# Unpacking of 4-bit weight codes: four operations in one step, or one behind each of four steps

## The reference, cut to what is computed

```python
xn = layernorm(x)
Wg, Wu, Wd = dequant(gate), dequant(up), dequant(down)   # 4-bit codes, two to an int32 word,
                                                         # scale per block of 32
gate, up = xn @ Wg.T, xn @ Wu.T                          # 2048 x 2048 each
g = tanh(0.79788 * (gate + 0.044715 * gate**3)) * gate * 0.5 + gate * 0.5
ffn = (g * up) @ Wd.T
attn = causal_attention(xn; 16 heads of 128)             # with its q, k, v, o projections
out = x + attn + ffn
```

## Time and profile before

| | us |
|---|---|
| median of 3 runs | 1382.64 |
| lowest, highest | 1381.21, 1383.4 |
| span of the traced execution | 1378.4 |
| feed-forward loop in it, with its start | about 42 to 345 |
| PE busy in it | 1301.3 |
| DVE, ACT, POOL busy in it | 960.6, 802.6, 792.9 |

### The profile page before, as it was taken

How to read it: one execution, slowest core, us unless ns; L and a number is a source line. 1 busy time by engine, 2 the same in 40 slices (tenths; PEclk the granted TensorE clock), 3 DMA queues, 4 the chain that set the end, 5 groups by cost and what they waited for, 6 DMA issues and landing times.

```text
span 1378.4 us, 25462 instructions
## 1 busy us (share of the span) xinstructions
PE 1301.3 (94%) x7628; PEld 1091.0 (79%) x7628; DVE 960.6 (70%) x1489; ACT 802.6 (58%) x1720; POOL 792.9 (58%) x799
## 2 busy tenths in 40 slices
PE   3899999998989999999999999999999999999996
PEld 2677777776668888878888887788888868888885
DVE  7777778887756666677665767766666686676665
ACT  3556555555366666645666665466666636666663
POOL 5566666666065576543656675266655715566563
PEclk9899999999999999999999999999999999999999
DMA  4000000000200000011000001100000020000003
GB/s 94 14 7 12 13 11 11 11 26 0 81 15 19 18 11 12 11 54 31 12 11 23 11 11 30 53 11 11 11 19 15 11 61 12 22 11 11 11 23 122
DMA packets 68144, 33.07 MB, mean 24 GB/s; under 512 B 17552, under 2 KB 68112, under 8 KB 68112
## 3 DMA queue, kind: packets, MB, share of 16 engines
q10 hardware_dynamic: 42544, 23.01, 5.8%
q1 hardware_dynamic: 25568, 9.66, 2.7%
HBM read 30.57 MB, written 2.10 MB: 24 GB/s over the span
## 4 chain that ended last, share of the span: by engine, by line
PE 68%; DVE 2%; issue 2%; ACT 1%; POOL 1%; DMA 1%; ACTq 0%; DVEq 0%; POOLq 0%
PE ps L43 19%; PE ps L45 18%; PE ps L44 18%; PE ps L1106 9%; PE ps L1045 2%; PE ps L1096 1%; DVE q_all L933 1%; DMA q_all<-in_x 1%; DVE neg_max L989 0%; POOL probs L878 0%; DVE v_lo L906 0%; DVE wq_lo L917 0%; POOL inv_sum L874 0%; POOL q_lo L854 0%; ACT pt_hi L781 0%
## 5 line engine op out<-in xcount | busy, mean ns | idle before, releaser
L951 DVE TENSOR_TENSOR pt_lo<-ps,pt_hi 128x512 fp32r<-128x512 f32 (+3 forms) x384 | 204.0, 552 | 275.4 <-ACT pt_hi L781 272.8
L874 POOL TENSOR_TENSOR inv_sum<-row_sum,minus_one 128x1 f32<-128x1 f32 x256 | 141.5, 553 | 379.2 <-ACT probs L795 379.2
L878 POOL TENSOR_TENSOR probs<-probs,inv_sum 128x128 f32<-128x128 f32 (+7 forms) x256 | 294.1, 1149 | 20.0
L795 ACT ACTIVATE probs<-ps,neg_max 128x128 f32<-128x128 f32 (+7 forms) x256 | 190.1, 743 | 115.7 <-DVE neg_max L989 111.6
L989 DVE TENSOR_REDUCE neg_max<-ps 128x1 f32<-128x128 f32 (+7 forms) x256 | 191.8, 749 | 4.6 <-PE ps L1096 2.4
L781 ACT ACTIVATE pt_hi<-ps 128x512 fp32r<-128x512 f32 (+3 forms) x384 | 173.4, 488 | 34.9 <-PE ps L1106 34.8
L44 PE MATMUL ps<-pt_lo,v_hi 128*128 128x256 f32 (+1 forms) x640 | 177.6, 278 | 0.0
L45 PE MATMUL ps<-pt_hi,v_lo 128*128 128x256 f32 (+1 forms) x640 | 177.6, 277 | 0.0
L43 PE MATMUL ps<-pt_hi,v_hi 128*128 128x256 f32 (+1 forms) x640 | 173.8, 272 | 0.7 <-DVE pt_lo L951 0.7
L1106 PE MATMUL ps<-ident,probs 128*128 128x128 f32 x1152 | 171.0, 275 | 1.6 <-POOL probs L878 0.6
L43 PE MATMUL ps<-k_hi,q_hi 128*128 128x512 f32 (+3 forms) x384 | 142.7, 372 | 2.6 <-DVE q_lo L942 2.2
(11 more groups left out here) (106 smaller groups left out, 3140.5 us busy)
## 6 DMA issues: line engine op xcount, KB each, us to landing
wq_in<-in_wq ACTq DMA_DIRECT2D x67, 128.0 KB, 2.2
kv_in<-in_wk ACTq DMA_DIRECT2D x33, 128.0 KB, 2.3
kv_in<-in_wv ACTq DMA_DIRECT2D x33, 128.0 KB, 2.2
wo_in<-in_wo ACTq DMA_DIRECT2D x33, 128.0 KB, 2.0
q_all<-in_x SPq DMA_DIRECT2D x1, 2048.0 KB, 8.8
out<-q_all SPq DMA_DIRECT2D x8, 256.0 KB, 2.3
raw<-in_gate SPq DMA_DIRECT2D x18, 64.0 KB, 1.8
raw<-in_up SPq DMA_DIRECT2D x18, 64.0 KB, 1.9
```

The source lines that it names most:

```text
L795: nc.scalar.activation(probs[:, t % 4, 0:width], flat(S[t % 2])[:, 0:width], ACT.Exp, bias=neg_max[:, t:t + 1], accum_out=row_sum[:, t:t + ...
L874: nc.gpsimd.tensor_tensor(inv_sum[:, t:t + 1], row_sum[:, t:t + 1], minus_one[:], ALU.pow).then_inc(inv_done, 1)
L878: nc.gpsimd.tensor_tensor(row, row, inv_sum[:, t:t + 1].to_broadcast([P, (i + 1) * P]), ALU.mult).then_inc(probs_done, 1)
L951: nc.vector.tensor_tensor(pt_lo[where], T[at % 2][:, 0:blocks * P].rearrange("p (a b) -> p a b", b=P), pt_hi[where].bitcast(F32), ALU.subt ...
```

## The change

`integers` becomes four calls of `integer(j, slot, part)`: parts 0 and 1 make `mag` (low and high code), parts 2 and 3 `sgn`. In the loop the call of `integers` is gone; in place of it each step ends with one part, behind `hid` and ahead of `w_lo`: part (kk + 1) % 4 of chunk it * 4 + 3 + (kk + 1) // 4. So part 0 of a chunk is behind step kk % 4 == 3, parts 1 to 3 behind the three steps after it. Part 0 of chunk 3 stands ahead of the loop; the last step has none, so the last 16 steps become a third copy of `body` on DVE and the loop has two turns. A new semaphore, `mag_done`, is counted up behind part 1, `ints_done` behind part 3. ACT's `over4` (part 0 of `linear`) waits for `mag_done`, its `half_sign` (part 3) for `ints_done`. DVE waits ahead of part 0 for the codes and for ACT's third operation on the last `mag`, and ahead of part 2 for the fourth, on the last `sgn`. No other queue's text changes; what is computed is the same.

```diff
--- before.py
+++ after.py
@@ -140,8 +140,8 @@
         offsets_set, stats_done, mean_done, eps_done, rstd_done, rows_done = (
             sem(s) for s in ("offsets_set", "stats_done", "mean_done", "eps_done", "rstd_done", "rows_done"))
         xt_done, xt_hi_done, xt_lo_done = sem("xt_done"), sem("xt_hi_done"), sem("xt_lo_done")
-        ints_done, linear_done, vals_done, w_rows_done = (
-            sem(s) for s in ("ints_done", "linear_done", "vals_done", "w_rows_done"))
+        mag_done, ints_done, linear_done, vals_done, w_rows_done = (
+            sem(s) for s in ("mag_done", "ints_done", "linear_done", "vals_done", "w_rows_done"))
         wt_done, wt_hi_done, wt_lo_done = sem("wt_done"), sem("wt_hi_done"), sem("wt_lo_done")
         gu_done, sq_done, inner_done, th_done, gated_done, hid_done = (
             sem(s) for s in ("gu_done", "sq_done", "inner_done", "th_done", "gated_done", "hid_done"))
@@ -286,6 +286,8 @@
 
                 for part in parts:
                     if part == 0:
+                        act.wait_ge(mag_done, j + 1)
+                    if part == 3:
                         act.wait_ge(ints_done, j + 1)
                     wait(act, vals_done, j * 3 - (2, 2, 1, 0)[part])
                     if part == 0:
@@ -355,16 +357,28 @@
 
         @block.vector
         def _(dve):
+            def integer(j, slot, part):
+
+                if part == 0:
+                    dve.wait_ge(raw_in[slot], (j >> 1) * 48 + 48)
+                    wait(dve, linear_done, j * 4 - 1)
+                if part == 2:
+                    wait(dve, linear_done, j * 4)
+                dst, mask = ((mag, 7), (sgn, 8))[part // 2]
+                pairs = dst[:].rearrange("p (k two) -> p k two", two=2)
+                if part % 2 == 0:
+                    ins = nc.vector.tensor_scalar(pairs[:, :, 0], raw[:, slot, :], mask, None, ALU.bitwise_and)
+                else:
+                    ins = nc.vector.tensor_scalar(pairs[:, :, 1], raw[:, slot, :], 4, mask,
+                                                  ALU.logical_shift_right, ALU.bitwise_and)
+                if part == 1:
+                    ins.then_inc(mag_done, 1)
+                if part == 3:
+                    ins.then_inc(ints_done, 1)
+
             def integers(j, slot):
-
-                dve.wait_ge(raw_in[slot], (j >> 1) * 48 + 48)
-                wait(dve, linear_done, j * 4)
-                for dst, mask in ((mag, 7), (sgn, 8)):
-                    pairs = dst[:].rearrange("p (k two) -> p k two", two=2)
-                    nc.vector.tensor_scalar(pairs[:, :, 0], raw[:, slot, :], mask, None, ALU.bitwise_and)
-                    last = nc.vector.tensor_scalar(pairs[:, :, 1], raw[:, slot, :], 4, mask,
-                                                   ALU.logical_shift_right, ALU.bitwise_and)
-                last.then_inc(ints_done, 1)
+                for part in range(4):
+                    integer(j, slot, part)
 
             def weights_low(j, slot):
                 dve.wait_ge(wt_hi_done, j + 1)
@@ -431,7 +445,7 @@
                     last = nc.vector.tensor_tensor(acc[:, :, cols], D, acc[:, :, cols], ALU.add)
                 last.then_inc(acc_done, 1)
 
-            def body(it, first):
+            def body(it, first, last=False):
                 for kk in range(BODY):
                     s, k1 = kk % 2, it * BODY + (kk + 1)
                     dve.wait_ge(sq_done, k1)
@@ -440,8 +454,6 @@
                                                    ).then_inc(inner_done, 1)
                     if kk % 2 == 1 and not (first and kk == 1):
                         add_down((kk - 3) // 2 % TC, it * GROUPS + (kk - 1) // 2, first and kk < 2 * TC + 3)
-                    if kk % 4 == 0:
-                        integers(it * 4 + (3 + kk // 4), (3 + kk // 4) % 2)
                     dve.wait_ge(th_done, k1)
                     nc.vector.scalar_tensor_tensor(gated[:, s, :], th[:, s, :], 1.0, G[s], ALU.add, ALU.mult
                                                    ).then_inc(gated_done, 1)
@@ -451,11 +463,16 @@
                                                    ALU.mult).then_inc(hid_done, 1)
                     if first and kk == 0:
                         xn_low(3)
+                    if not (last and kk == BODY - 1):
+                        m = (kk + 1) // 4
+                        integer(it * 4 + (3 + m), (3 + m) % 2, (kk + 1) % 4)
                     if kk % 4 == 3:
                         weights_low(it * 4 + (2 + kk // 4), (2 + kk // 4) % 4)
+            integer(3, 1, 0)
             body(0, True)
-            with dve.Fori(1, NJ // 4) as it:
+            with dve.Fori(1, NJ // 4 - 1) as it:
                 body(it, False)
+            body(NJ // 4 - 1, False, True)
             add_down(TC - 1, NJ // 4 * GROUPS, False)
 
         @block.tensor

```

## The result

The changed kernel takes 1361.56 us (median of 4 runs, 1361.07 to 1362.04) where the kernel before takes 1382.9 beside it: ratio 0.9849, 95% interval 0.9837 to 0.9861. The traced execution has a span of 1359.7 us where that of before has 1378.4: 18.7 us less. The forecast was 1362.5 us, from 20.1 us less.

The account below looks back on a forecast made before the run. PE was taken as the bound, so a pass gains only what PE waits. 15 passes x 1.25 = 18.8 us, plus 1.3 at the start, gives 20.1: 1382.64 - 20.1 = 1362.5 us, range 1359.5 to 1371.

Parts of the forecast that it names:

- a distance of 4.2 us: Median of the runs, 1382.64, above the traced span, 1378.4, before the change; the forecast left it unchanged.
- PE waits for `hid` once a pass: Feed-forward loop, step 2: PE's wait costs 1.25 us of an 18.66 us pass; without it 17.41.
- Why the unpackings are long: DVE ahead of `hid`: two unpackings take 1.47 and 2.00 us against POOL's `hid_lo` and `vals`, 0.35 when free.
- The pass laid out by hand: Times of the new pass on each engine from step 0's start, with PE at 0, 4.19, 8.38, 13.14 and 17.41.
- The step that failed: Part 0 behind step 3: held by `vals` to about 3.34, `w_lo` about 3.27, `inner` 4.24 instead of 3.63.
- the loop's term: Feed-forward loop: the stall goes in every pass, 15 passes x 1.25 = 18.8 us.
- The start: First steps: part 0 of chunk 3 loses to `vals`, yet `hid` comes at 45.65 instead of 46.93; gain 1.3, bounds 0 to 1.7.
- Rival 1's margin: Step 1: later `mag_done` uses up 1.17 us, half the gain returns, 1371.9; together with its worst end 0.15.
- Rival 4: Part 1 blocked through `hid_lo` and `w_rows` to 11.14; 2.05 lost for 1.25 won per pass, 1394.6; chance 0.06.
- The Trainium skill's rule: DVE and POOL's shared ports: speaks against spreading, since each part now meets POOL; dearest pass is four full blocks.

Follow-up runs that it names:

- run 1: The changed kernel with `w_lo` ahead of part 0 behind step 3: 1359.97 us, ratio to the kernel before 0.9844.
- run 4: The kernel before, unpackings in their old place, POOL's third operation on `vals` (the sign) cut to 8 of 768 columns: 1356.77 us, one run.
- run 6: The kernel of run 1 with part 0 of chunk 3 between the first `inner` and `gated` instead of ahead of the loop: 1359.31 us, 0.9837.
- The repeat: The changed kernel, unaltered, measured once more for a comparison on one chip: 1362.48 us, ratio to the kernel before 0.9858.
- with six: The changed kernel with six added statistics operations on DVE ahead of part 1 in every pass but the start: 1374.23 us, one run.
- with nine: The changed kernel with nine added statistics operations on DVE ahead of part 1 in every pass but the start: 1390.29 us, one run.
- run 2: The kernel before with all four unpackings as one block, one count, moved behind `hid` of step 0: 1364.09 us, ratio 0.9866.
- run 3: The block of run 2 with two counts, one behind `mag` and one behind `sgn`: 1363.08 us, ratio to the kernel before 0.9865.

## Why the prediction was right, step by step

The mechanism and the size of the gain were right; that the time came within 0.9 us has luck in it. The trace lost 18.7 us, 1.4 less than the 20.1 forecast. Against that, the forecast kept a distance of 4.2 us from the span to the median, and measured it is 1.9 (1361.56 and 1359.7). Where an execution's own time and span are both known, they lie 1.7 to 1.9 apart, so the traced execution of the kernel before took about 1380.3 us by this estimate and was faster than its median. The two errors take most of each other away.

- *PE waits for `hid` once a pass, worth 1.25 us, and the next latest is PE itself.* Right but for `w_lo` (below): 17.41 us in a pass without a late start, and the floor that runs 1, 4 and 6 share is a loop of 273.7: 292.66 - 273.7 = 18.96 us, 15 times 1.26.
- *Why the unpackings are long: they stand against POOL.* Right; run 4 cuts the POOL operation short and the unpacking is short (0.36 instead of 2.00).
- *The pass laid out by hand.* Measured from 196.98: part 0 at 2.66 (laid out 2.66), `w_lo` 3.27 (3.27), `inner` 4.14 (4.24), `hid` 6.23 (6.33), part 1 6.83 (6.93), `over` 8.21 (8.2), `hid` of step 1 11.23 (11.23), part 3 15.20 (15.2). A pass of a steady loop can be laid out from start-to-start distances.
- *The step that failed:* "`w_lo` starts about 3.27 [...] Cost on DVE 0.61 us", which went on to `inner` and stopped there. `w_lo` has a second reader: PE's gate/up of step 1 waits for it whenever it takes up a new chunk, and that starts at 4.19, when `w_lo` ends at 4.2. The forecast priced who is queued behind the held operation on its engine and not who waits for it. Mis-sized by it is the loop's term: 15 x 1.25 = 18.8, of which 17.6 came; the seven starts behind `w_lo` cost 1.39 us by run 1, and the wait itself was worth 19.0.
- *The start.* Forecast 1.3, measured 1.29 (13.59 to 12.30). `inner` came at 43.41 where 43.56 was laid out, `hid` at 45.51 (45.65). In this trace PE's slow stretch covers the late `mag_done`, as the forecast had it: `hid` is issued at 51.51, and step 3 starts at 52.65, more than 0.74 behind. The repeat has 11.95: its slow stretch lies earlier, and PE waits 0.95 us for `hid` in the first step 3. The exact hit has some luck in it.
- *The third copy of `body` on DVE* cost nothing: PE has no wait for `hid` anywhere in the loop.
- *Rival 1's margin* (step 1's `hid`, 1.17 us behind `mag_done`) has a twin that the forecast didn't list: `add_down` of step 1, queued on DVE behind part 1, feeds PE's down group of step 2, with about 1.3 us to spare. When part 1 is later by two or three microseconds both are missed, PE meets `acc` first, and what it waits there it doesn't wait in step 3. The size follows the forecast's own rule, free up to 9.4 us in the pass and one for one beyond: `mag_done` at 9.89 with six gives 0.5 (measured 0.7), at 11.34 in the held passes with nine 1.9 (measured 2.1).
- *Rival 4* (slower): its price for a pass was right, 15.2 to step 3 and measured 15.23, and its cause takes more than POOL's queue. With part 1 held to the end of `w_rows` in 9 of 15 passes the kernel is slower than before (1390.29 against 1381.61 beside it), but only with 3 us of added work ahead of it.
- *The Trainium skill's rule,* SBUF — State Buffer, "Who interferes with whom": the first to issue holds the shared pair for its whole instruction. This case agrees: 0.69, 0.69 and 0.78 in the changed kernel, 1.08 with six, each ending about 0.2 behind POOL's operation; 1.57 behind `w_rows`; and `w_rows` longer by 0.11 to 0.25 where DVE was first. That each part now met POOL on its own cost time only where a part's follower had no margin; here one had none.

## What to carry to other kernels

Take work that nobody needs yet out of the chain that the busiest engine waits for; where it goes matters more than whether it is split (a block of four in the right place gave the same loop). When an operation is moved, list for each one behind it both its queue followers and the readers of its result, with the time at which each reader needs it, and put those with an early reader ahead of the moved part. The start is a case of its own: the block that was free in the loop gained nothing there, and PE's wait behind it was followed by a slow clock.

## What the hardware showed that was not expected

- A DVE operation that contends with POOL can be served at the border of two POOL operations even when POOL's next is already queued: in 6 of the 15 passes with nine, part 1 took 0.34 to 0.39 us and the `w_rows` behind it 1.60 to 1.74 instead of 1.49. Once it was listed 0.05 us behind the start of `w_rows` (205.82 and 205.77), and in another pass, 0.06 behind, it was held (1.64 us). The listed start of a POOL operation is thus no proof that it holds the ports.
- The granted clock at the start varies between traces of one kernel (0.70 in 45 to 50 us in one, 1.00 there and 0.70 in 40 to 45 in the other), and the first step 3 moves by 0.35 us with it.
- In the loop the clock stayed at 1.00 behind waits of 1.0 to 1.1 us in every pass (before) and of 0.35 (with six). It fell to 0.50 for 5 us behind a wait of 3.10 (run 2) and to 0.71 behind one of 2.46 (run 3). Waits of 1.79 to 2.07 were followed by slow clock in 3 of 9 passes (with nine). Two of those three waits were 1.79, as in most of the six passes where it stayed at 1.00; the runs don't show what decides.
